# Second attention of a five-stage network: operations of the prologue reordered and moved between engines, reciprocals formed on ScalarE, the first sequence's tensors stored in six transfers

## The chip, the core and the metric

The kernel runs on one core of a Trainium2 chip. Its engines work side by side, each through its own list of instructions, and wait for each other by semaphores: TensorE (PE; its weight loads are PEld), VectorE (DVE), ScalarE (ACT), GpSimd (POOL) and SyncE (SP), which here only issues DMAs. TensorE's clock is granted at 1.2 or 2.4 GHz, in the profile 0.5 or 1. The metric is the device time of one execution, in microseconds.

## The reference, cut to what matters

The network computes, on x of shape (4, 1024, 128), attention a, a feed-forward block, attention b, a second feed-forward block with the same weights, each on a layer norm of x and added to x. The change is in attention b (16 heads of 8 channels, 4 sequences of 1024 tokens):

```python
Q, K, V = (split_heads(jnp.einsum('bsd,od->bso', x, W)) for W in (Wq, Wk, Wv))
Q, K = _apply_rope(Q, cos, sin), _apply_rope(K, cos, sin)
logits = jnp.einsum('bhnd,bhmd->bhnm', Q, K) * scale
probs = jax.nn.softmax(jnp.where(causal, logits, -jnp.inf), axis=-1)
attn = jnp.einsum('bhnm,bhmd->bhnd', probs, V).swapaxes(-3, -2).reshape(*x.shape[:-1], D)
return jnp.einsum('bsd,od->bso', attn, Wo)
```

## The kernel before

`network` runs five stages one after the other; `attn_b_stage` is the third. X lies in SBUF with the 128 channels on the partitions and 4 x 1024 tokens along them.

**Norm.** X is normed in eight chunks c of 512 tokens, two to a sequence b: TensorE centres (`centre`, L1527), ScalarE squares (L1727), TensorE averages (`mean`, L1536), ScalarE forms the reciprocal root by a logarithm and an exponential (`rstd`, L1733, L1735), VectorE multiplies (`normed`, L1845). Two banks alternate.

**Q and K.** For each sequence b and w (0 is Q, 1 is K) four products (`product`, L1549) give the projection and that of the swapped channels, i = 0 and 1, into two banks of 1024 columns. The rope is two multiplications by tables and an addition. For b = 0 VectorE does them from PSUM (L1853, L1856); for b = 1, 2, 3 ScalarE first copies the banks to SBUF (`hold`, L1753; into TA and TB, for b = 2 into XN and XE) and GpSimd multiplies and adds (`turn_and_add`, L1966, L1969). The sum is cut into three bf16 parts: first part a copy by ScalarE (L1740), remainder (L1861 or L1975), second part by ScalarE (L1744), third part (L1866 or L1980). `store_parts` (L1461) writes all three to DRAM by one DMA per tensor, and `load(m)` (L1471, L1476) brings group m of four heads back, three DMAs for each of QS and KS, into a ring of three. `value_product` (L1557) gives V, copied by ScalarE (L1758).

**Scores twice.** There are 16 groups m, four to a sequence. First each query's maximum is found: max units on TensorE (L1606 mask, L1609 scores) into two banks, reduced by VectorE (L1884). When the maximum of a group is known (L1894), GpSimd splits it (`offsets`, L2002 to L2008), TensorE turns it (L1618), VectorE casts it (L1901), SyncE writes it into QS as three further rows (`rows`, L1496). Then exp units compute the transposed scores with that offset (L1635, L1640), ScalarE takes the exponential (L1816), and the value products (L1655) sum outputs and denominators. Step n, 0 to 15, has eight slots j: exponentials of group n, tiles j, with maxima of group n + 1 (slots 0 to 3) and n + 2 (slots 4 to 7) between. The cast of group n + 1 is in slot 5 of step n; the casts mark the steps below. During steps -2 and -1, where there are only maxima, the 18 projection pieces of sequences 2 and 3 lie between them.

**Output.** ScalarE copies each half output to OS (`copy_out`, L1805), and `store_out` moves numerators (L1489, into OA) and denominators (L1491, into DA) by 8 small DMAs into the place of the rope tables; for the first two sequences it waits until all rope work is done (L1485). Step 4b + 5 closes sequence b: four reciprocals of 256 columns (`denominators`, L1907), two scalings (`scale`, L1912), two output products (L1664), added to X (L1919). Sequence 3 is closed behind the last step.

The order within each engine is written by hand: the calls at the end of each engine's block.

## Time and profile before

| | us |
|---|---|
| median of 3 runs | 2334.87 (2330.69 to 2345.4) |
| the profiled execution | 2331.8 |
| its span, first to last instruction | 2330.0 |
| TensorE busy (matmuls) | 2106.8 |
| VectorE busy | 1815.8 |
| ScalarE busy | 1386.5 |
| GpSimd busy | 1175.6 |

The second attention lies at about 915 to 1587 us of the span. In the rows further down a time in brackets is how long the engine stood idle before the row, and the arrow names what ended that; "x8" is the number of instructions that a row gathers; SPq is SyncE's issue of DMAs.

### The profile page before, as it was taken

The page shows a single profiled execution, that of the slowest core. Times are in us where ns is not written, and L with a number is a line of the kernel's source. Part 1 is how long each engine was busy: PE and PEld are TensorE (multiplying, and loading weights), DVE is VectorE, ACT ScalarE, POOL GpSimd, SP SyncE. Part 2 cuts the span into 40 slices and gives each one's busy share as a digit, 9 for nine tenths or more (in the row PEclk, how much of TensorE's full clock was granted, in tenths as well). Part 3 has the DMA queues.
Part 4 walks back from the last instruction along what each step waited for, and adds up shares of the span by engine and source line. Part 5 has one row for each costly group of instructions (what it writes and reads, how often), then busy time and mean ns, then how long its engine had stood idle before and what let it go on. Part 6 is the DMA issues. An engine that isn't in the chain of part 4 may idle for free. (4 is left out here: it accounts for less than half of the span.)

```text
span 2330.0 us, 45158 instructions
## 1 busy us (share of the span) xinstructions
PE 2106.8 (90%) x16918; PEld 1085.9 (47%) x16918; DVE 1815.8 (78%) x2394; ACT 1386.5 (60%) x3463; POOL 1175.6 (50%) x533
## 2 busy tenths in 40 slices
PE   5687899999999998787999989996899999999997
PEld 2233555555555553332333333333455555555553
...
GB/s 60 0 1 82 69 33 42 42 33 46 33 42 42 33 33 51 89 54 31 74 51 33 47 49 44 35 12 78 71 37 37 43 36 44 37 35 45 34 36 42
DMA packets 85564, 101.16 MB, mean 43 GB/s; under 512 B 13305, under 2 KB 59329, under 8 KB 83045
## 3 DMA queue, kind: packets, MB, share of 16 engines
q1 hardware_dynamic: 82981, 96.64, 15.6%
q8 instruction: 137, 2.24, 0.4%
...
## 5 line engine op out<-in xcount | busy, mean ns | idle before, releaser
L831 POOL TENSOR_TENSOR ffn_RN<-ffn_SS,ffn_mhalf 128x16 f32<-128x16 f32 x128 | 372.5, 2910 | 282.3 <-DVE ffn_SS L777 281.8
L1884 DVE TENSOR_REDUCE attn_b_NX<-attn_b_s 128x1 f32<-128x512 f32 (+3 forms) x608 | 384.4, 659 | 152.9 <-PE attn_b_s L1609 148.5
L1816 ACT ACTIVATE attn_b_PT<-attn_b_s 128x1024 f32<-128x1024 f32 (+3 forms) x352 | 298.3, 870 | 237.3 <-PE attn_b_s L1640 232.7
L825 POOL TENSOR_TENSOR ffn_QK<-ffn_T 128x1024 f32<-128x1024 f32 x128 | 421.4, 3292 | 19.9 <-DVE ffn_T L725 19.6
L576 ACT ACTIVATE ffn_PB<-ffn_s,ffn_NM 128x128 f32<-128x128 f32 x1024 | 359.9, 385 | 102.2 <-DVE ffn_NM L747 102.2
L612 ACT ACTIVATE ffn_SQ<-ffn_w 128x1024 f32<-128x1024 f32 x128 | 131.0, 1024 | 311.8 <-DVE ffn_T L725 311.5
L819 POOL TENSOR_TENSOR ffn_PB<-ffn_PB,ffn_RDEN 128x1024 f32<-128x1024 f32 x128 | 243.7, 1904 | 23.7 <-DVE ffn_RDEN L710 23.7
L367 PE MATMUL ffn_w<-ffn_Wqkv,ffn_H 128*128 128x512 f32 x512 | 245.4, 602 | 9.1 <-ACT ffn_SQ L612 5.6
L1609 PE MATMUL attn_b_s<-attn_b_KS,attn_b_QS 72*128 72x512 bf16 (+3 forms) x768 | 223.8, 339 | 12.8 <-DVE attn_b_NX L1884 9.7
L576 ACT ACTIVATION_READ_ACCUMULATOR ffn_PB<-ffn_s,ffn_NM 128x1 f32 x1024 | 230.9, 225 | 0.0
L741 DVE TENSOR_TENSOR ffn_QK<-ffn_QK,ffn_RN 128x1024 f32<-128x1024 f32 x128 | 221.4, 1730 | 0.4 <-POOL ffn_RN L831 0.3
L764 DVE COPY ffn_PT<-ffn_w 128x1024 f32<-128x1024 f32 x128 | 156.2, 1220 | 75.1 <-PE ffn_w L421 71.7
L442 PE MATMUL ffn_m<-ffn_HN,ffn_W 128*114 128x512 f32 x360 | 185.9, 613 | 6.6 <-ACT ffn_G L596 4.1
L1640 PE MATMUL attn_b_s<-attn_b_QS,attn_b_KS 75*128 75x512 bf16 (+3 forms) x768 | 190.3, 337 | 0.0
L722 DVE TENSOR_TENSOR ffn_T<-ffn_w,ffn_rope 128x1024 f32<-128x1024 f32 x128 | 154.8, 1210 | 36.3 <-PE ffn_w L367 36.1
L1655 PE MATMUL attn_b_o<-attn_b_PT,attn_b_VQ 128*32 128x512 f32 (+3 forms) x1536 | 170.7, 517 | 0.1
L747 DVE TENSOR_REDUCE ffn_NM<-ffn_s 128x8 f32<-128x1024 f32 x128 | 155.5, 1215 | 11.5 <-PE ffn_s L409 11.5
L725 DVE TENSOR_TENSOR ffn_T<-ffn_w,ffn_rope 128x512 f32<-128x512 f32 x256 | 163.6, 681 | 0.0
L774 DVE TENSOR_REDUCE ffn_SS<-ffn_SQ 128x16 f32<-128x1024 f32 x128 | 154.6, 1208 | 2.2 <-ACT ffn_SQ L612 2.2
L437 PEld LDWEIGHTS ffn_w<-ffn_PT,ffn_Voff 128*64 128x64 f32 x2048 | 107.3, 137 | 101.1 <-issue 94.6
L421 PEld LDWEIGHTS ffn_w<-ident,ffn_PB 128*128 128x128 f32 x1024 | 116.5, 142 | 74.8 <-issue 60.2
L367 PEld LDWEIGHTS ffn_w<-ffn_Wqkv,ffn_H 128*128 128x128 f32 x512 | 95.0, 193 | 117.3 <-issue 82.4
(242 smaller groups left out, 3801.0 us busy)
## 6 DMA issues: line engine op xcount, KB each, us to landing
...
attn_b_rope<-attn_b_OS SPq DMA_DIRECT2D x256, 16.0 KB
```

The source lines that it names most:

```text
L367: last = pe.matmul(w0_ps[:, c, :], H1[:, g % 2, b, :], Wqkv[:, l, c, :], start=True, stop=True)
L442: pe.matmul(mlp_bank(g, half, j), W1[:, g // NT, half, j, :], HN[:, :], start=True, stop=True)\
L576: last = act.activation(PB[:, x % 2, e, p, :], s_ps[:, e, p * P:(p + 1) * P], ACT.Exp, bias=NM[:, x % 2, e, p:p + 1], accum_out=DEN[:, x % ...
L741: dve.tensor_tensor(qk, qk, RN[:, x % 2, :].unsqueeze(2).broadcast_to([P, 2 * NH, DH]), ALU.mult)\
L819: pool.tensor_tensor(probs_x, probs_x, by, ALU.mult).then_inc(normed, 1)
L825: pool.tensor_tensor(QK[:, x % 2, :, :, :].rearrange("p c q k -> p (c q k)"), T1[:, :, :, :].rearrange("p c h k -> p (c h k)"), T2[:, :, : ...
L831: pool.tensor_tensor(RN[:, x % 2, :], SS[:, x % 2, :], mhalf[:, :], ALU.pow).then_inc(rnorm, 1)
L1609: last = pe.matmul(bank[:, q * width:(q + 1) * width], QS[0:KS9, m % RING, g + q, i * P:(i + 1) * P], KS[0:KS9, m % RING, g + q, lo:hi], s ...
L1640: last = pe.matmul(bank[:, q * pitch + lo:q * pitch + hi], KS[:, n % RING, g + q, j * P:(j + 1) * P], QS[:, n % RING, g + q, j * P + lo:j ...
L1655: last = pe.matmul(o_ps[half][VCOLS * g:VCOLS * (g + 1), lo - half * 512:512], VQ[:, n % 2, g, j, :], PT[:, j % 2, g, lo - j * P:hi - j * ...
L1816: act.activation(PT[:, j % 2, g:g + pack, 0:width], s2_ps[k % 2][:, 0:pack * pitch].rearrange("p (q w) -> p q w", q=pack)[:, :, 0:width], ...
L1884: dve.tensor_reduce(NX[:, m % 2, c, g:g + pack, i], s1_ps[k % 2][:, 0:pack * (hi - lo)].rearrange("p (q w) -> p q w", q=pack), AX_X, ALU.m ...
```

## The change

The diff, cut to its core (adapted thresholds of waits are left out, except in `store_out`):

```diff
+    def store_part(b, w, a):
+        sp.wait_ge((p1, p2, p3)[a], 2 * b + w + 1)
+        sp.dma_start(qk_dram[w][a, b * P:(b + 1) * P, :], RP[:, w, a, :]).then_inc(s_parts_out[w], 16)
...
         else:
-            sp.wait_ge(turned, 8)
-            sp.wait_ge(rotated, 4 * (NB - 1))
+            sp.wait_ge(turned, 16)
+            sp.wait_ge(rotated, 4 * (NB - 2))
         cols = slice(half * 512, (half + 1) * 512)
         for g in range(BG):
-            to = slice(n % 4 * 32 + g * BD, n % 4 * 32 + (g + 1) * BD)
-            sp.dma_start(OA[to, b % 2, cols], OS[32 * g:32 * g + BD, n % 2, cols])\
+            sp.dma_start(DA[rows_of(n, g), b % 2, cols], OS[32 * g + BD:32 * g + 2 * BD, n % 2, cols])\
               .then_inc(s_back[half][n % 2], 16)
-            sp.dma_start(DA[to, b % 2, cols], OS[32 * g + BD:32 * g + 2 * BD, n % 2, cols])\
-              .then_inc(s_back[half][n % 2], 16)
+        if (n, half) != (NG - 1, 1):
+            for g in range(BG):
+                sp.dma_start(OA[rows_of(n, g), b % 2, cols], OS[32 * g:32 * g + BD, n % 2, cols])\
+                  .then_inc(s_back[half][n % 2], 16)
...
-    for w in range(2):
-        store_parts(0, w)
+    for a in range(PARTS):
+        for w in range(2):
+            store_part(0, w, a)
     for m in range(RING):
...
     rows(0)
-    for w in range(2):
-        store_parts(2, w)
     for n in range(NG):
...
             store_out(n - 1, 1)
-        if n + 1 < NG:
-            rows(n + 1)
-        store_out(n, 0)
         if n == 2:
...
                 store_parts(3, w)
+        if n + 1 < NG:
+            rows(n + 1)
+        if n >= 1:
+            store_out(n, 0)
         if n + RING < NG:
...
             load(n + RING)
+        if n == 0:
+            for w in range(2):
+                store_parts(2, w)
+            store_out(0, 0)
     store_out(NG - 1, 1)
...
         pe.wait_ge(s_w, 16 * WLOADS)
-        pe.wait_ge(n_ln, min(2 * b + 4, NCH))
+        pe.wait_ge(n_ln, NCH if b else 4)
         wait(pe, v_copied, 2 * b)
...
         mean(c)
-    projections(0, 0)
+    projections(0)
     for c in range(2, 4):
         centre(c)
-    projections(0, 1)
+    projections(1)
     for c in range(2, 4):
...
     value_product(0)
-    for c in range(4, 6):
+    for c in range(4, 8):
+        w, h = divmod(c - 4, 2)
         centre(c)
-    projections(1, 0)
-    for c in range(4, 6):
+        for i in range(2):
+            product(1, w, i, h)
         mean(c)
-    projections(1, 1)
-    for c in range(6, 8):
-        centre(c)
     value_product(1)
-    for c in range(6, 8):
-        mean(c)
     pe.wait_ge(n_out, NCH)
...
         square(c)
-    for c in range(2, 4):
-        rstd(c)
+    rstd(2)
     first_part(0, 1)
...
         second_part(0, w)
+    rstd(3)
     copy_values(0)
-    for c in range(4, 6):
+    for c in range(4, 8):
         square(c)
-    for c in range(4, 6):
         rstd(c)
-    hold(1, 0)
-    hold(1, 1)
-    for c in range(6, 8):
-        square(c)
+    first_part(1, 0)
     copy_values(1)
-    for c in range(6, 8):
-        rstd(c)
+    first_part(1, 1)
     hold(2, 0)
     for w in range(2):
-        first_part(1, w)
+        second_part(1, w)
+    hold(2, 1)
     copy_values(2)
-    hold(2, 1)
-    for w in range(2):
-        second_part(1, w)
     for w in range(2):
...
     copy_values(3)
-    for w in range(2):
-        first_part(2, w)
     act.wait_ge(n_out, NCH)
...
+    def inverse(b, half):
+        cols = slice(half * 512, (half + 1) * 512)
+        for i in range(2):
+            act.wait_ge(s_back[half][i], 32 * BG * (2 * b + 2))
+        act.activation(DA[:, b % 2, cols], DA[:, b % 2, cols], ACT.Ln).then_inc(s_lden, 1)
+        act.wait_ge(s_lden, 2 * b + half + 1)
+        act.activation(DA[:, b % 2, cols], DA[:, b % 2, cols], ACT.Exp, scale=-1.0).then_inc(s_rden, 1)
...
                     for w in range(2):
+                        first_part(2, w)
+                if (n, j, g) == (0, 6, 0):
+                    for w in range(2):
                         second_part(2, w)
-                if (n, j, g) == (1, 1, 1):
+                if (n, j, g) == (1, 5, 0):
                     for w in range(2):
                         first_part(3, w)
-                if (n, j, g) == (2, 1, 1):
+                if (n, j, g) == (1, 7, 0):
                     for w in range(2):
                         second_part(3, w)
+                if n % 4 == 1 and n > 1 and j in (2, 3) and g == 0:
+                    inverse(n // 4 - 1, j - 2)
                 if (j, g) == (5, 0):
...
     copy_out(NG - 1, 1)
+    act.wait_ge(o_read[1], NG)
+    act.wait_ge(s1_mm, s1_at["out", NB - 3, 1] + 1)
+    for g in range(BG):
+        act.dma_start(OA[rows_of(NG - 1, g), (NB - 1) % 2, 512:], OS[32 * g:32 * g + BD, (NG - 1) % 2, 512:])\
+           .then_inc(s_back[1][(NG - 1) % 2], 16)
+    for half in range(2):
+        inverse(NB - 1, half)
...
+    def turn(b, w, i, h):
+        half = slice(h * 512, (h + 1) * 512)
+        dve.wait_ge(ab_mm, 8 * b + 4 * w + (2 * h + i if b else 2 * i + h) + 1)
+        wait(dve, p3, (w + 1) * b)
+        dve.tensor_tensor((TA, TB)[i][:, w, half], s2_ps[i][:, half], rope[:, 2 * w + i, half], ALU.mult)\
+           .then_inc(turned, 1)
...
         dve.wait_ge((s_wq, s_wk)[w], 16 * 4)
-        for i, dst in enumerate((TA, TB)):
+        for i in range(2):
             for h in range(2):
-                half = slice(h * 512, (h + 1) * 512)
-                dve.wait_ge(ab_mm, 4 * w + 2 * i + h + 1)
-                dve.tensor_tensor(dst[:, w, half], s2_ps[i][:, half], rope[:, 2 * w + i, half], ALU.mult)\
-                   .then_inc(turned, 1)
+                turn(0, w, i, h)
         dve.wait_ge(turned, 4 * w + 4)
...
         remainder(w)
+    normed(2)
     for w in range(2):
         third_part(w)
-    for c in range(2, NCH):
+    normed(3)
+    for c in range(4, NCH):
+        w, h = divmod(c - 4, 2)
+        for i in range(2):
+            turn(1, w, i, h)
         normed(c)
...
-    def denominators(b, lo, hi):
-        half = lo // 512
-        for i in range(2):
-            dve.wait_ge(s_back[half][i], 32 * BG * (2 * b + 2))
-        dve.reciprocal(DA[:, b % 2, lo:hi], DA[:, b % 2, lo:hi]).then_inc(s_rden, 1)
...
             for b in closing:
-                if 1 <= slot <= 4:
-                    denominators(b, 256 * (slot - 1), 256 * slot)
                 if slot in (5, 6):
                     scale(b, slot - 5)
-            if n == NG - 1 and slot == 6:
-                denominators(NB - 1, 0, 256)
-                denominators(NB - 1, 256, 512)
-                scale(NB - 1, 0)
         if n == NG:
-            denominators(NB - 1, 512, 768)
-            denominators(NB - 1, 768, 1024)
-            scale(NB - 1, 1)
+            for half in range(2):
+                scale(NB - 1, half)
         for b in range(NB):
...
+    def add(b, w, a, c):
+        pool.tensor_tensor(a, a, c, ALU.add).then_inc(rsum, 1)
...
     def turn_and_add(b, w):
-        pool.wait_ge((s_wq, s_wk)[w], 16 * 4)
-        k = 4 * (b - 1) + 2 * w
-        for i, at in enumerate(work_buffers(b, w)):
+        k = 4 * (b - 2) + 2 * w
+        a, c = work_buffers(b, w)
+        for i, at in enumerate((a, c)):
             pool.wait_ge(held, k + i + 1)
             pool.tensor_tensor(at, at, rope[:, 2 * w + i, :], ALU.mult).then_inc(rotated, 1)
-        a, c = work_buffers(b, w)
         pool.wait_ge(rotated, k + 2)
-        pool.tensor_tensor(a, a, c, ALU.add).then_inc(rsum, 1)
+        add(b, w, a, c)
...
     for w in range(2):
-        turn_and_add(1, w)
+        pool.wait_ge(turned, 8 + 4 * w + 4)
+        add(1, w, *work_buffers(1, w))
     parts_of(1)
-    for w in range(2):
-        turn_and_add(2, w)
+    turn_and_add(2, 0)
     for m in range(NG):
         offsets(m)
-        if m + 1 < NG:
-            values(m + 1)
         if m == 0:
+            values(1)
+            turn_and_add(2, 1)
+        elif m == 1:
             parts_of(2)
-        if m == 1:
             for w in range(2):
                 turn_and_add(3, w)
-        if m == 2:
-            parts_of(3)
+            values(2)
+        else:
+            if m == 2:
+                parts_of(3)
+            if m + 1 < NG:
+                values(m + 1)
```

TensorE takes chunks 4 to 7 one at a time, with two products of sequence 1 behind each centring, and the values of sequence 1 after the last mean. VectorE does the rope multiplications of sequence 1 itself; GpSimd only adds. In ScalarE's prologue the copies change places, and the copies of parts of sequences 2 and 3 now stand among the exponentials of steps 0 and 1.

On ScalarE, the order behind the chunks 2 and 3 of the norm (RP is the buffer of the parts, VB of the values). Before:

```order
L1733 ACTIVATE attn_b_PT<-attn_b_o,eps 128x512
L1735 ACTIVATE attn_b_PT<-attn_b_PT 128x512
L1733 ACTIVATE attn_b_PT<-attn_b_o,eps 128x512
L1735 ACTIVATE attn_b_PT<-attn_b_PT 128x512
L1740 ACTIVATE attn_b_RP<-attn_b_TA 128x1024
L1744 ACTIVATE attn_b_RP<-attn_b_TA 128x1024 x2
L1758 ACTIVATE attn_b_VB<-attn_b_o 128x4x4x32 x2
```

Now:

```order
L1743 ACTIVATE attn_b_PT<-attn_b_o,eps 128x512
L1745 ACTIVATE attn_b_PT<-attn_b_PT 128x512
L1750 ACTIVATE attn_b_RP<-attn_b_TA 128x1024
L1754 ACTIVATE attn_b_RP<-attn_b_TA 128x1024 x2
L1743 ACTIVATE attn_b_PT<-attn_b_o,eps 128x512
L1745 ACTIVATE attn_b_PT<-attn_b_PT 128x512
L1768 ACTIVATE attn_b_VB<-attn_b_o 128x4x4x32 x2
```

The root of chunk 3 has moved behind the three copies of parts.

On GpSimd, the work of sequence 2 (in XN and XE) around the offsets of group 0 (NP, NR). Before:

```order
L1966 TENSOR_TENSOR attn_b_XN<-attn_b_XN,attn_b_rope 128x1024 x2
L1969 TENSOR_TENSOR attn_b_XN<-attn_b_XN 128x1024
L1966 TENSOR_TENSOR attn_b_XE<-attn_b_XE,attn_b_rope 128x1024
L1966 TENSOR_TENSOR attn_b_XN<-attn_b_XN,attn_b_rope 128x1024
L1969 TENSOR_TENSOR attn_b_XE<-attn_b_XE,attn_b_XN 128x1024
L2002 TENSOR_TENSOR attn_b_NP<-attn_b_NM,attn_b_zeros 128x32
```

Now:

```order
L1986 TENSOR_TENSOR attn_b_XN<-attn_b_XN,attn_b_rope 128x1024 x2
L1979 TENSOR_TENSOR attn_b_XN<-attn_b_XN 128x1024
L2021 TENSOR_TENSOR attn_b_NP<-attn_b_NM,attn_b_zeros 128x32
L2023 TENSOR_TENSOR attn_b_NR<-attn_b_NM,attn_b_NP 128x32
L2025 TENSOR_TENSOR attn_b_NP<-attn_b_NR,attn_b_zeros 128x32
L2027 TENSOR_TENSOR attn_b_NP<-attn_b_NR,attn_b_NP 128x32
L2011 COPY attn_b_VQ<-attn_b_VB 128x8x4x8
L1986 TENSOR_TENSOR attn_b_XE<-attn_b_XE,attn_b_rope 128x1024
```

K's three operations have moved behind the offsets.

On SyncE, steps 0 and 1, now (before, the eight stores of group 0's first half output stood ahead of the loads, and sequence 2's parts ahead of both):

```order
L1504 DMA attn_b_QS<-attn_b_MT 3x32x128 x2
L1478 DMA attn_b_QS<-attn_b_qk_parts 24x1x4096 x3
L1483 DMA attn_b_KS<-attn_b_qk_parts 24x1x4096 x3
L1464 DMA attn_b_qk_parts<-attn_b_RP 128x3x1024 x2
L1495 DMA attn_b_rope<-attn_b_OS 8x512 x4
L1499 DMA attn_b_rope<-attn_b_OS 8x512 x4
...
L1504 DMA attn_b_QS<-attn_b_MT 3x32x128
```

The load of group 3 stands ahead of the stores into the rope tables; two half outputs are stored before the offsets of group 2.

## Rows read from the trace of the kernel before

**Rows 1.** The page's first line.

```profile
span 2330.0 us, 45158 instructions
```

**Rows 2.** Timeline 910 to 1012 us: start, duration, engine, line, operation, [idle before <-releaser].

```profile
933.84 0.67 ACT L1733 ACTIVATE attn_b_PT<-attn_b_o,eps 128x512 f32<-128x512 f32 x1
934.54 0.63 ACT L1735 ACTIVATE attn_b_PT<-attn_b_PT 128x512 f32<-128x512 f32 x1
...
934.65 2.02 PE L1557 MATMUL attn_b_o<-attn_b_Wv,attn_b_XN 128*128 128x128 f32 x16 [1.25 <-ACT attn_b_PT L1733]
935.08 1.04 ACT L1740 ACTIVATE attn_b_RP<-attn_b_TA 128x1024 bf16<-128x1024 f32 x1
...
940.38 3.54 PE L1527 MATMUL attn_b_s<-X,centre 128*128 128x512 f32 x4 [3.70 <-DVE attn_b_XN L1845]
...
943.75 3.60 PE L1549 MATMUL attn_b_s<-attn_b_XN,attn_b_W 128*128 128x512 f32 x8
...
947.18 1.88 PE L1536 MATMUL attn_b_o<-attn_b_PT,mean 128*128 128x512 f32 x4
...
964.82 0.23 PE L1606 MATMUL attn_b_s<-attn_b_causal,identb 128*128 128x128 bf16 x1 [2.55 <-DVE attn_b_XN L1845]
```

**Rows 3.** Timeline 969 to 1012 us, to the first exponential's mask matmul (last row).

```profile
985.23 1.10 PE L1549 MATMUL attn_b_s<-attn_b_XN,attn_b_W 128*128 128x512 f32 x2 [1.63 <-ACT attn_b_XE L1753]
...
998.28 2.35 DVE L1894 TENSOR_TENSOR attn_b_NM<-attn_b_NX 128x32 f32<-128x32 f32 x1
...
1002.96 2.34 POOL L1969 TENSOR_TENSOR attn_b_XE<-attn_b_XE,attn_b_XN 128x1024 f32<-128x1024 f32 x1
...
1006.62 0.31 PE L1618 MATMUL attn_b_s<-identb,attn_b_NP 128*96 128x128 bf16 x1 [3.71 <-POOL attn_b_NP L2008]
...
1011.02 0.31 PE L1635 MATMUL attn_b_s<-attn_b_causal,identb 128*128 128x128 bf16 x1
```

**Rows 4.** Stretches: length, busy us of PE, PEld, DVE, ACT, POOL; clock, DMA share, GB/s.

```profile
955.00:960.00 5.00, 4.06 (x22) 2.67 (x20) 0.00 (x0) 3.02 (x5) 4.92 (x3) 1.00 0.19 79
...
985.00:990.00 5.00, 4.20 (x15) 1.87 (x16) 2.60 (x5) 3.71 (x5) 2.98 (x2) 1.00 0.15 64
...
1010.00:1020.00 10.00, 9.90 (x35) 4.33 (x34) 5.67 (x9) 5.21 (x6) 0.97 (x1) 0.50 0.01 2
```

**Rows 5.** Timeline of steps 1 and 2, 1054 to 1125 us.

```profile
1066.10 1.06 ACT L1740 ACTIVATE attn_b_RP<-attn_b_TA 128x1024 bf16<-128x1024 f32 x1 [5.95 <-POOL attn_b_TA L1969]
...
1068.02 0.29 PE L1635 MATMUL attn_b_s<-attn_b_causal,identb 128*128 128x128 bf16 x1 [9.80 <-ACT attn_b_PT L1816]
...
1069.27 2.24 SPq L1471 DMA_DIRECT2D attn_b_QS<-attn_b_qk_parts  x3
...
1087.35 0.39 PE L1635 MATMUL attn_b_s<-attn_b_causal,identb 128*128 128x128 bf16 x2 [4.84 <-DMA attn_b_KS<-attn_b_qk_parts]
...
1100.15 0.60 ACT L1816 ACTIVATE attn_b_PT<-attn_b_s 128x512 f32<-128x512 f32 x1 [0.97 <-PE attn_b_s L1640]
...
1101.07 0.22 PE L1635 MATMUL attn_b_s<-attn_b_causal,identb 128*128 128x128 bf16 x1
```

**Rows 6.** Stretches from cast to cast of the offsets (L1901), columns as in rows 4.

```profile
1095.40:1127.60 32.20, 31.41 (x243) 12.51 (x242) 24.38 (x41) 21.01 (x27) 9.76 (x9) 1.00 0.15 47
1193.50:1233.40 39.90, 35.11 (x245) 13.38 (x242) 30.55 (x45) 20.77 (x27) 1.39 (x5) 0.91 0.12 38
1333.60:1371.00 37.40, 32.00 (x244) 12.39 (x242) 30.31 (x45) 20.64 (x27) 1.38 (x5) 1.00 0.13 40
1469.70:1511.20 41.50, 37.85 (x244) 14.44 (x242) 30.43 (x45) 20.51 (x27) 1.39 (x5) 0.84 0.11 36
1041.80:1095.40 53.60, 38.39 (x245) 14.12 (x242) 24.85 (x42) 21.38 (x28) 15.29 (x11) 0.81 0.09 28
```

**Rows 7.** Timeline of the tail, 1565 to 1600 us.

```profile
1577.47 0.62 SPq L1491 DMA_DIRECT2D attn_b_rope<-attn_b_OS  x1
...
1579.53 3.36 DVE L1907 RECIPROCAL attn_b_rope<-attn_b_rope 128x256 f32<-128x256 f32 x2 [1.30 <-DMA attn_b_rope<-attn_b_OS]
```

30 lines of the change are left out of this document (17 added, 13 removed).

## The prediction

> **What bounds the kernel now.** I read the page's head first (a span of 2330.0 us; the run took 2331.8, so 1.8 us lie around it) [rows 1]. Only one of five stages is touched, the second attention, about 915 to 1587 us. There I read the timeline stretch by stretch, each time for the wait that ends last. It falls into four pieces. (a) A prologue: the norm's chunks travel ScalarE to VectorE to TensorE and back, and TensorE waits 3.70 us for the third chunk and 2.55 us for the last one; it begins the first scores at 964.8 us [rows 2]. (b) From there to the first exponential at 1011.0 us: the maximum of group 0 is started at 998.28, but GpSimd is in the middle of six multiplications and additions of sequence 2 and is free only at 1005.3 us, so TensorE waits 3.71 us for the offsets [rows 3]. (c) Sixteen steps. An ordinary one takes 32.2 us with TensorE busy for 31.41 of them [rows 6]: TensorE bounds it, and whatever makes it wait is lost. Step 0 to 1 takes 53.6 us instead [rows 5]: TensorE stands 9.80 us because ScalarE waits for GpSimd's sum of sequence 3, and 4.84 us for the load of group 3. Those are one chain: SyncE may store group 0's output over the rope tables only when GpSimd has finished with them, and the load (issued at 1069.27) is queued behind those stores [rows 5]. (d) Three closing steps with four reciprocals of 1.7 us on VectorE each, and a tail behind the last stores [rows 6, 7].
>
> **The change part by part.** Times below are times of the old trace, moved.
>
> Prologue. ScalarE: the second half of the reciprocal roots of chunk 3 (a logarithm and an exponential, 0.67 + 0.63 us) no longer stands before the first part of K, which started at 935.08 [rows 2]; it starts when the roots of chunk 2 end, 933.9. The chain of first part, VectorE's remainder, second part and third part then ends near 938.1 (Q) and 939.3 (K) instead of 938.5 and 939.7. Chunk 2 is normed between, at 936.9. The price is that the values of sequence 0 now wait for chunk 3's logarithm: TensorE's idle time is 4.65 us (933.4 to 938.05), then 2.0 us of values, and the fifth chunk's centring starts at 940.1, where it started at 940.38 [rows 2]. From there the two schedules differ. Per chunk TensorE now has one centring, two products and one mean, four pieces like the four products that now start at 943.75 and are followed 3.43 us later (947.18) by the means [rows 2]: 3.43 us. ScalarE has three operations and VectorE three per chunk, of 0.6 to 0.7 us each (2.1 at most), so TensorE bounds it: 4 x 3.43 = 13.7 us. The clock is granted at half speed after the idle time of 3.70 us now (two centrings took 3.54 us at 940.38, two means 1.88 at full speed [rows 2]), and I keep that loss of 1.7 us. Last mean at 940.1 + 13.7 + 1.7 = 955.5; the values of sequence 1 wait 0.75 us for the last logarithm and take 2.0: first scores at 958.3. Now 964.8: a gain of **6.5 us**. VectorE's eight rope multiplications replace four evacuations of 1.0 us on ScalarE and four multiplications of 2.35 us on GpSimd.
>
> Cover that can be gone: the scores need the load of group 0. Loads move at 79 GB/s, 0.19 of the DMA capacity, until 985 to 990 us, when the rate falls [rows 4]; they are issued from 942.1, so three take 47 us, one 15.6, and group 0 is there at 957.7, if they land in order; at the latest at 964.5, since nothing waited for it. The six small stores should let it start 1.3 us earlier (last part on its way at 939.3, a third of the bytes). Needed at 958.3: 1.9 us to spare, or 4.9 us short at the far bound (964.5 - 1.3 - 958.3). I take nothing, since the nearest reading is the measured rate.
>
> To the first exponential. The evacuation of sequence 2's K now stands before the copy of its values (1.1 us), and TensorE's 1.63 us wait for it [rows 3] shrinks by that. GpSimd now has only three operations of sequence 2 between the parts of sequence 1 (done near 973) and the offsets: it is idle when the maximum is ready. So the maximum starts at 998.3 - 6.5 - 1.1 = 990.7, and need not take 2.35 us for its 32 elements, an operation that now overlaps GpSimd's; five reductions of some 0.65 us later, at 993.8, TensorE turns the offsets, and it reaches the first exponential 4.4 us after that, as now (1006.62 to 1011.02): 998.2 [rows 3]. Gain so far **12.8 us**.
>
> Step 0 ran at half clock for most of its first 12 us (0.50 from 1010 to 1020 [rows 4]). From the first exponential to the next cast it took 30.8 us (1011.0 to 1041.8); at full clock the same stretch takes 26.5 (from 1101.07 [rows 5] to the cast at 1127.6 that ends the first window of rows 6). Gain **4.3**, together 17.1.
>
> Step 1. GpSimd after the change: sequence 2's third parts end 9.2 us after cast 1 (that cast now at 1024.7), six operations of 2.35 us end at 1048; ScalarE needs the sum at 1057, 9 us later: no wait. SyncE issues the load of group 3 at 1031, ahead of the stores: landed by about 1050 (18 us from issue to the end of the wait now, 1069.3 to 1087.35 [rows 5]), needed at 1053. So 53.6 becomes 32.2: gain **21.4**. The stores of two half outputs (16 issues of 0.62 [rows 7] and a little between them, 10.7 us from 1045.5) end at 1056.2, and the offsets' row of group 2 is queued behind them and wanted at 1057.
>
> What is moved onto ScalarE costs something. Two copies (2.1 us) beside the exponentials were free in step 2: they stand in the window of 32.2 us whose ScalarE time is 21.01 [rows 6]. But now pairs stand at the end of steps 0 and 1, where the idle time before an exponential is 0.97 us [rows 5]: 2.1 - 0.97 = 1.1, of which step 0 loses perhaps half, and in step 1 a second pair delays the head pair of tile 5 too. I take 0.5 + 1.7 = **2.2 us lost** (bounds 0 and 4.4).
>
> Closing steps. They take 39.9, 37.4 and 41.5 us [rows 6]; against 32.2 the three lose 22.1 us. Reciprocals alone are 4 x 1.7 = 6.8 each; the rest is half clock in two of them (0.91, 0.84 [rows 6]). Now ScalarE does two logarithms and two exponentials, 2 x (0.67 + 0.63) = 2.6 us [rows 2], the size of the pair that was free. Bounds: nothing, and 2.6 each; I take 0.8 each, so the gain is 22.1 - 2.4 = **19.7** (14.3 to 22.1). The closing's other half (scalings, output product) stays.
>
> A rule against this change: the Trainium skill (DMA: Bandwidth & Descriptors, section Bandwidth) advises transfers of at least 1 MiB and measures 138 GB/s at 64 KB; at that rate a 256 KB part takes 1.9 us. By it the sum changes by at most the 1.3 us of earlier start, which lies in the cover; no row of the kernel before shows a transfer of that size.
>
> Tail. Two reciprocals (3.36 us) follow the last of eight store issues (1577.47; they begin 2.06 us later, when it has landed) [rows 7], and a scaling of 0.7 ends at 1583.6. Four of the issues go to ScalarE's queue, so SyncE's last comes 4 x 0.65 = 2.6 us earlier; logarithm and exponential (1.3) replace 3.36. Gain 2.6 + 2.0 = **4.6**.
>
> Sum: 17.1 + 21.4 - 2.2 + 19.7 + 4.6 = 60.6, and 2331.8 - 60.6 = 2271.2. The run of the profile lies 3.1 us under the median shown (2334.87), which one long run raises; I forecast 2272.
>
> **The rivals.** (1) ScalarE's insertions cost what they last: 4.4 and 2.6 x 3 instead of 2.2 and 2.4, so 7.6 us less gain: about 2280. For it: an exponential that comes late delays the value product behind it. Against: the window of 32.2 with 21.01 us of ScalarE [rows 6]. (2) The clock: TensorE's idle time ahead of the values grows to 4.65 us, and half speed stays or returns where I have it full, in the chunks (1.7 us more), in step 0 (4.3) and in one closing (4.1, the third over the second, 41.5 - 37.4): about 2282. (3) The load of group 0 is the bound: up to 4.9 us: 2277. (4) The queue behind the moved stores: if GpSimd runs 3.9 us later than I have it, the offsets' row of group 2 is late, and each further us is lost; ten later would be 6: 2278. (5) The change doesn't remove the reciprocals' cost, since TensorE waits for its score banks anyway: then 19.7 falls away, 2292. Against it: ordinary steps take 32.2 and the middle closing, at full clock, 5.2 more. (6) Slower: the new mix keeps TensorE at 1.2 GHz through the steps. In step 0, 12 us at half clock cost 4.3, so they did 7.7 us of work, and a whole step of 32.2 would take 50; it decides from three and a half steps on (60.6 / 18), and with five the kernel is 1% slower, 2361. Rows 6 show a whole step at 1.00, which is against it.
>
> **How the numbers follow.** As forecast 0.63; (1) 0.13, (2) 0.10, (3) 0.05, (4) 0.03, (5) 0.04, (6) 0.02. The range goes from 2260 (no insertion costs anything, 4.6 off; the half clock of the chunks gone too, 1.7; the closings that follow a half-clocked one also freed of it, some 4) to 2289, which leaves out (5), (6) and a sum of (1) with (2). A change of 1%, 23 us, is about what a measurement of this kernel can tell from none. Faster by over 1% (under 2311.5): 0.95; within 1%: 0.03; slower: 0.02.
>
> **What the profile after would show.** First scores at 958, first exponential at 998, cast 1 at 1025, cast 2 at 1057.5; maximum 0 of 0.19 us; no wait of TensorE over 2 us in step 1; closing windows of 32 to 35 us at clock 1.00; the tail's last scaling 4.6 us earlier relative to the last exponential. I am wrong if the first scores wait for a DMA, if step 1 is still above 36 us, or if the closings keep more than 4 us each.

## The result, and the profile after

Over four executions the changed kernel has a median of 2275.18 us (2273.19 to 2283.85); the kernel before, timed beside it, 2339.16 (2330.69 to 2345.4). The ratio is 0.9736, 95% interval 0.9692 to 0.9779: 2.2 to 3.1% faster. Forecast were 2272 us and a range of 2260 to 2289.

The first profile of the changed kernel happened to be its longest execution (2283.85), so I took a second one (`r1_again`, 2275.14; six executions, median 2275.32). Their heads:

```profile
span 2282.1 us, 45155 instructions
PE 2099.0 (92%) x16918; PEld 1085.6 (48%) x16918; DVE 1792.8 (79%) x2386; ACT 1391.9 (61%) x3475; POOL 1166.3 (51%) x529
```

```profile
span 2273.3 us, 45155 instructions
PE 2091.5 (92%) x16918; PEld 1084.1 (48%) x16918; DVE 1792.4 (79%) x2386; ACT 1391.8 (61%) x3475; POOL 1166.1 (51%) x529
```

Same instructions, and TensorE busy 7.5 us longer in the first: that is clock, not work. The stage also begins at a slightly different time in each execution, because the stages ahead of it vary. So every mark below is counted from the stage's own first centring (915.78 us before, 918.62 and 917.14 in the two profiles after), and the stage ends where GpSimd clears its first tile of the next one (1587.75, 1538.31, 1529.15).

| from the stage's start, us | before | after, 1st | after, 2nd | gain, 2nd | forecast |
|---|---|---|---|---|---|
| first scores | 49.0 | 44.1 | 43.9 | 5.1 | 6.5 |
| scores for the first exponential | 95.2 | 84.9 | 84.7 | 10.5 | 12.8 |
| cast 1 | 126.1 | 115.7 | 115.5 | 10.5 | 17.1 |
| cast 2 | 179.6 | 147.9 | 147.8 | 31.8 | 38.5 |
| cast 3 | 211.8 | 187.2 | 181.0 | 30.8 | |
| cast 15 | 627.9 | 578.7 | 572.5 | 55.4 | |
| end of the stage | 672.0 | 619.7 | 612.0 | 60.0 | 60.6 |

The sum came out in the second profile, its terms didn't all: several missed by 1 to 4 us, in both directions. Over the first profile the stage gained 52.3 us. The other stages took 1658.0 us of the span before and 1661.3 in the second profile, with not one instruction changed there; over all 14 profiles of this study they take 1655.9 to 1662.4. That is 3.3 of the 3.9 us by which the second profile's execution lies above 2271.2; the other 0.6 are the stage's.

The windows of the first profile after, by cast as in [rows 6] (columns: start:end, length, busy time of PE, PEld, DVE, ACT and POOL, TensorE's granted clock, DMA share, GB/s). They are step 0, step 1, step 2, and the three steps in which the first closings fall:

```profile
999.40:1034.30 34.90, 33.46 (x199) 13.07 (x199) 24.43 (x41) 18.33 (x21) 8.19 (x8) 0.80 0.01 2
1034.30:1066.60 32.30, 31.42 (x244) 12.55 (x242) 24.48 (x42) 21.28 (x28) 21.03 (x14) 1.00 0.27 95
1066.60:1105.90 39.30, 37.61 (x244) 14.09 (x242) 24.55 (x42) 23.09 (x30) 9.81 (x9) 0.83 0.23 79
1170.30:1202.80 32.50, 31.53 (x245) 12.55 (x242) 24.50 (x42) 21.58 (x30) 1.38 (x5) 1.00 0.14 46
1301.40:1333.80 32.40, 31.43 (x243) 12.56 (x242) 24.39 (x41) 21.48 (x29) 1.39 (x5) 1.00 0.15 47
1432.50:1464.90 32.40, 31.43 (x244) 12.56 (x242) 24.40 (x42) 21.48 (x30) 1.38 (x5) 1.00 0.14 46
```

Read the clock (third from the right) first. Step 1 (53.60 before, now 32.30) and the closings (39.90, 37.40, 41.50, now 32.4 to 32.5) are at 1.00, with TensorE busy for all but 0.9 to 1.0 us: they are ordinary steps now. Step 0 is at 0.80 and as long as before (34.9). Step 2 is at 0.83 here and takes 39.30; in the second profile the same instructions take 33.30 at clock 1.00:

```profile
1064.90:1098.20 33.30, 31.48 (x244) 12.55 (x242) 24.46 (x42) 23.03 (x30) 9.77 (x9) 1.00 0.27 94
```

### The profile page after: what moved, and what is told of

It is laid out like the page before. It is cut to its first block and busy times, and to the rows that moved or that the text cites. A ratio compares the mean times of both kernels' runs of the same rounds, so it can differ in the third digit from the quotient of the medians.

```text
span 2282.1 us, 45155 instructions
## 1 busy us (share of the span) xinstructions
PE 2099.0 (92%) x16918; PEld 1085.6 (48%) x16918; DVE 1792.8 (79%) x2386; ACT 1391.9 (61%) x3475; POOL 1166.3 (51%) x529
## 5 line engine op out<-in xcount | busy, mean ns | idle before, releaser
L1619 PE MATMUL attn_b_s<-attn_b_KS,attn_b_QS 72*128 72x512 bf16 (+3 forms) x768 | 219.1, 334 | 5.8 <-DVE attn_b_NX L1914 2.5
L367 PEld LDWEIGHTS ffn_w<-ffn_Wqkv,ffn_H 128*128 128x128 f32 x512 | 95.2, 193 | 120.0 <-issue 82.6
```

The source lines that it names most:

```text
L367: last = pe.matmul(w0_ps[:, c, :], H1[:, g % 2, b, :], Wqkv[:, l, c, :], start=True, stop=True)
L1619: last = pe.matmul(bank[:, q * width:(q + 1) * width], QS[0:KS9, m % RING, g + q, i * P:(i + 1) * P], KS[0:KS9, m % RING, g + q, lo:hi], s ...
```

## The experiments

Each is one edit of the changed kernel unless said otherwise. They ran in three groups on the same chip, each beside the kernel before: the first four below (kernel before 2329.34 us); the reciprocals, the two transfers, the stores ahead of the load and the two fillings together (2330.88); the filling in the kernel before, the later GpSimd, the third filling and the load in pieces (2328.88). Where a time is compared with the changed kernel's, that is its median of 2275.32 from the first group.

### The same kernel once more

> The changed kernel as it is, a second profile of it. The first one lay 8.7 us over its own median (2283.85 against 2275.18) and shows TensorE at half clock in two stretches of the steps, 1001.6 to 1015.2 us (step 0) and 1076.7 to 1090.3 us (end of step 2's first tiles; cast 2 to cast 3 took 39.30 us where an ordinary step takes 32.24). Theory A: the half clock belongs to what the engines do there, so both stretches come back at the same places (within 1 us of the casts beside them), and the windows cast 0 to 1 and cast 2 to 3 are again 34.9 and 39.3 us. Theory B: the two stretches are chance; then a profile near 2275 us lacks one of them, and its window is 32.2 to 32.5 us. Median 2275 us in either.

Median 2275.32, ratio 0.9763 (0.9736 to 0.979). Half clock of step 0: there again (14 us, from 1.4 us behind cast 0); half clock of step 2: absent. So both theories hold, one for each place. With the runs below, step 0 took 34.8 to 35.7 us in all nine profiles whose TensorE has nothing added ahead of it (the kernel before among them), while step 2, in seven with the pair of copies in tile 7 of step 1, took 33.25 three times, 36.19, 36.20, 36.32, and 39.30. (The eighth with that pair is the run with GpSimd later, whose step 2 holds a further wait.)

### Second parts of sequence 3 later

```diff
-                        if (n, j, g) == (1, 7, 0):
+                        if (n, j, g) == (2, 1, 1):
                             for w in range(2):
                                 second_part(3, w)
```

> Only ScalarE's second parts of sequence 3 move, from tile 7 of step 1 to tile 1 of step 2, where the kernel before had them (the pair lasts 1.99 us; behind it TensorE waited 0.96 us at 1075.01 and went to half clock 1.7 us later, for 13.6 us). Theory A (ScalarE's pair behind the last tile is what makes TensorE stand, and the standing brings the half clock): cast 2 to cast 3 falls from 39.3 to 32.3 us and the kernel to 2268. Theory B (the pair costs what it lasts, the half clock comes from something else): the window loses 1 to 2 us at most, the half clock stays near 1077, the kernel 2274. Theory C (the pair in tile 1 meets the load and stores there): the window stays or grows.

Median 2271.4, 3.9 us under the changed kernel; the intervals of the two ratios overlap (0.9718 to 0.9776 here), so the windows must tell it. What the pair does in tile 7 shows in the second profile of the changed kernel (ScalarE, then TensorE; start, duration, and in brackets the idle time and what ended it):

```profile
1070.42 1.99 ACT L1754 ACTIVATE attn_b_RP<-attn_b_TA 128x1024 bf16<-128x1024 f32 x2
...
1073.38 0.23 PE L1645 MATMUL attn_b_s<-attn_b_causal,identb 128*128 128x128 bf16 x1 [0.95 <-ACT attn_b_PT L1825]
```

The pair stands in front of the next step's exponentials and TensorE stands 0.95 us. Moved by two tiles it has slack: step 2 takes 32.5 us, at full clock, in this and in the three other profiles with the pair there.

```profile
1063.80:1096.30 32.50, 31.45 (x244) 12.55 (x242) 24.43 (x42) 22.88 (x30) 9.76 (x9) 1.00 0.28 96
```

Theory A, with a correction: the pair costs 0.8 us each time, and in four of seven profiles a stretch of half clock follows, 2.9 to 6.1 us more. Against the second profile, which lacks that stretch, the move gains only the 0.8 us of theory B.

### Two more such pairs, and a third at the end

```diff
+                        if (n, j, g) in ((6, 7, 0), (10, 7, 0), (14, 7, 0)):
+                            for w in range(2):
+                                act.wait_ge(s_parts_out[w], 16 * (3 + PARTS))
+                                act.activation(RP[:, w, 1, :], TA[:, w, :], ACT.Copy)
```

> The changed kernel with work added: in steps 6, 10 and 14 ScalarE does, behind the exponential of tile 7, two more copies of 128x1024 into a buffer that nothing uses any more (the same 1.99 us at the same place as the second parts of sequence 3 in step 1). Theory A (such a pair there stops TensorE about 1 us and brings the half clock): the windows of casts 7 to 8, 11 to 12 and 15 on, 32.24 us each now, grow by 7 us each where the next step is whole, in all 14 to 21 us: about 2290. Theory B (a pair costs its wait only, the half clock has another cause): 0 to 1 us each, about 2277.

Median 2282.7, 7.4 us over the changed kernel: neither theory's number. The windows behind the first two of the added pairs:

```profile
1226.20:1262.10 35.90, 34.38 (x244) 13.44 (x242) 24.53 (x42) 21.08 (x28) 1.39 (x5) 0.90 0.13 42
1360.90:1393.90 33.00, 31.35 (x244) 12.55 (x242) 24.41 (x41) 21.20 (x27) 1.39 (x5) 1.00 0.14 46
```

One with a stretch of half clock (3.7 us over the ordinary 32.24), one without (0.8 us); the stretch from cast 15 to the stage's end is 3.7 longer than in the second profile, but some half clock comes there without a pair too (1.5 us in the first profile of the changed kernel). The same edit at the same place: a short stand of TensorE sometimes brings the half clock and sometimes not. No run here shows what decides it.

### Work for TensorE ahead of step 0

```diff
                             max_unit(m, *unit)
+                            if n == -1 and m == 1:
+                                pe.wait_ge(held, 4 * (NB - 2))
+                                for _ in range(2):
+                                    pe.matmul(s2_ps[0][:, 0:512], QS[0:KS9, 0, 0, 0:P], KS[0:KS9, 0, 0, 0:512],
+                                              start=True, stop=True, skip_group_check=True)
```

> The changed kernel with work added: behind each of the eleven score units of group 1 ahead of step 0, TensorE does two more products of 512 columns (0.22 us each at full clock) into a bank that the first exponential's scores overwrite. Nothing reads them. Between 995 and 1003 us TensorE was busy 3.7 to 4.4 of each 5 us, and its clock fell to half at 1001.6. Theory A (low work of TensorE ahead of step 0 brings its half clock): the half clock of step 0 goes, cast 0 to cast 1 falls from 34.9 to 31 or 32 us, less up to 2 us that the added products delay the score units; 2272 to 2275. Theory B (the half clock is set by something else, such as a fixed time behind the last one): cast 0 to cast 1 stays at 34.9 or grows by up to 3 us; 2275 to 2280.

(The added lines stand here in place of a helper.) Median 2268.86, 6.5 us under the changed kernel. First the 9 us of the second profile that end where its step 0 fell to half clock (999.2 us), and 9 us from some 30 us earlier; then the 9 us of this run that correspond to the first, and its step 0:

```profile
990.20:999.20 9.00, 7.31 (x44) 3.95 (x43) 6.93 (x14) 2.11 (x3) 5.15 (x7) 1.00 0.08 32
958.00:967.00 9.00, 6.80 (x38) 4.09 (x39) 4.89 (x8) 4.86 (x7) 6.16 (x3) 1.00 0.19 79
```

```profile
987.00:996.00 9.00, 8.53 (x55) 5.07 (x54) 6.71 (x14) 2.11 (x3) 5.80 (x7) 1.00 0.05 19
994.10:1024.20 30.10, 29.02 (x207) 11.74 (x207) 24.26 (x42) 17.71 (x22) 8.06 (x8) 1.00 0.01 2
```

TensorE busy for 8.53 instead of 7.31 of the 9 us, the other engines about as they were, and step 0 takes 30.1 us instead of 34.9. Theory A: filling the gaps takes the half clock away. That little busy time alone brings it is not shown, and the second line speaks against it: around 958 us TensorE was busy for 6.80 of 9 us, and its clock stayed full until 999.2. The score units were not delayed (cast 0 came 80.2 us from the stage's start, 80.6 without). The step in which I had expected 4.3 us from the clock held 4.8, and the change had not touched what brings them.

### The same in the kernel before

```diff
+                            if n == -1 and m == 1:
+                                filler(2)
...
                         if slot == TURN_SLOT and n == -1:
+                            filler(14)
                             turn_unit(0)
```

`filler(k)` is the same product k times.

> The kernel before with the same filling of TensorE ahead of step 0: two added products behind each of the eleven score units of group 1 and 14 ahead of the turning of group 0's offsets, where it stood 3.71 us. Theory A (step 0's half clock belongs to TensorE's idle time ahead of it, in both kernels, and the change neither made nor removed it): cast 0 to cast 1 falls from 34.87 to 30 or 31 us and the kernel gains 4 to 5 us. Theory B (in the kernel before something else lowers the clock in step 0): the window stays at 34.9 and nothing is gained.

```profile
1001.40 3.18 PE L1670 MATMUL attn_b_s<-attn_b_KS,attn_b_QS 72*128 72x512 bf16 x14
1005.09 0.23 PE L1618 MATMUL attn_b_s<-identb,attn_b_NP 128*96 128x128 bf16 x1 [0.51 <-POOL attn_b_NP L2017]
```

```profile
1005.40:1035.20 29.80, 28.86 (x206) 11.59 (x204) 24.17 (x41) 17.72 (x22) 9.26 (x8) 1.00 0.15 55
1035.20:1089.50 54.30, 39.84 (x244) 14.86 (x242) 24.77 (x41) 21.30 (x28) 15.29 (x11) 0.75 0.09 28
```

Step 0 falls from 34.87 to 29.8 us, as theory A has it: in this kernel too the half clock goes when the time ahead is filled. This run fills the gaps and the wait of 3.71 us together, so it doesn't say which of them brings the half clock in the kernel before. And the kernel gains only 1.1 us between the medians (ratio 0.9981, 0.9962 to 1.0), not the 4 to 5 of theory A, and not told from nothing. The profile shows where the 5 us go: the window of step 1 is 0.8 us longer than before, the first two closings 2.3 and 2.4, the step behind the second closing 1.6, while the third closing (3.0) and the step behind the first (1.6) are shorter; the half clock behind the waits falls differently.

### Reciprocals back on VectorE

```diff
-                        if n % 4 == 1 and n > 1 and j in (2, 3) and g == 0:
-                            inverse(n // 4 - 1, j - 2)
...
+                        if 1 <= slot <= 4:
+                            denominators(b, 256 * (slot - 1), 256 * slot)
...
```

The four reciprocals behind the last step are put back likewise.

> The changed kernel with VectorE's reciprocals back: four of 128x256 in each closing step and four at the end instead of ScalarE's logarithms and exponentials; everything else as changed. Theory A (my sum: the reciprocals cost 19.7 us in the closings beyond what ScalarE's way costs; by the windows of both profiles it would be 23.2: 39.88, 37.42 and 41.55 against 32.43 each): the windows of casts 5 to 6, 9 to 10 and 13 to 14 are 37 to 42 us again, with half clock near one or two of them, the tail 2 to 3 us longer, the kernel 2294 to 2300. Theory B (TensorE waited for its banks anyway, the reciprocals cost little): windows within 1 us of 32.4, kernel 2278.

Median 2300.61, ratio 0.9864 (0.9839 to 0.9889): the stage takes 635.8 us, 23.8 more than in the second profile. The three closing windows:

```profile
1162.70:1201.70 39.00, 33.56 (x244) 12.87 (x242) 30.40 (x46) 20.71 (x27) 1.39 (x5) 0.96 0.12 39
1300.30:1340.20 39.90, 35.11 (x244) 13.35 (x242) 30.55 (x46) 20.77 (x27) 1.40 (x5) 0.91 0.11 38
1440.40:1477.80 37.40, 31.98 (x244) 12.38 (x242) 30.32 (x45) 20.63 (x27) 1.40 (x5) 1.00 0.12 40
```

VectorE is busy 6 us longer than in the same windows after (30.4 against 24.4 to 24.5) and does four instructions more, reciprocals of 1.74 us each; at full clock that costs 5.0 us a step, and 6.6 and 7.4 where the half clock follows. Together with 1.6 in the step behind the second closing that is 20.6, and 3.2 in the tail. Theory A; its 2294 to 2300 us for the kernel was missed by 0.6.

### Two transfers for the first sequence

```diff
-            for a in range(PARTS):
-                for w in range(2):
-                    store_part(0, w, a)
+            for w in range(2):
+                store_parts(0, w)
```

> The changed kernel with the first sequence's parts stored in two transfers of 768 KB in all three parts again, each behind its third part, instead of six of one part. Theory A (my prediction: the load of group 0 starts 1.3 us later and has about 2 us of cover): the first scores start 0 to 1 us later, the kernel is within 1 us of 2275. Theory B (the first scores wait for the load; in the first profile of the changed kernel they did so for 0.68 us): they start 1.3 us or more later, up to 4 if the large transfers land later, and the kernel is 2276 to 2279.

Median 2276.48 (2275.31 to 2281.9), ratio 0.9766 (0.9744 to 0.9789): not to be told from the changed kernel by time. The profile tells it. First scores and load of group 0 in the changed kernel (first profile), then here:

```profile
944.85 2.32 SPq L1478 DMA_DIRECT2D attn_b_QS<-attn_b_qk_parts  x3
962.70 0.22 PE L1616 MATMUL attn_b_s<-attn_b_causal,identb 128*128 128x128 bf16 x1 [0.68 <-DMA attn_b_KS<-attn_b_qk_parts]
```

```profile
942.36 2.32 SPq L1474 DMA_DIRECT2D attn_b_QS<-attn_b_qk_parts  x3
960.50 0.22 PE L1611 MATMUL attn_b_s<-attn_b_causal,identb 128*128 128x128 bf16 x1 [2.51 <-DMA attn_b_KS<-attn_b_qk_parts]
```

With this stage's start at 914.58 the load is issued 27.8 us from it, against 26.2 in the first profile of the changed kernel and 24.2 in most others (see below), and TensorE waits 2.51 instead of 0.68 us. Theory B: in this one profile the first scores come 45.9 us from the start, against 43.1 to 44.1 with six transfers, so these are worth 1.8 to 2.8 us there. This profile also has a further stretch of half clock behind that wait (its cast 0 comes 4.7 us later), which its median does not show. That the third parts' stores land later in some executions is taken up in the part on the prediction.

### Stores ahead of the load

```diff
                 if n + 1 < NG:
                     rows(n + 1)
-                if n >= 1:
-                    store_out(n, 0)
+                store_out(n, 0)
```

> The changed kernel with one place of the store queue as before: group 0's first half output is stored ahead of the load of group 3, not behind it; GpSimd's order stays the new one. The stores over the rope tables may start when GpSimd's last multiplication of sequence 3 ends, about 21 us after cast 1, so the load is issued 26 us after cast 1 and landed 18 us later, where TensorE wants it about 20 us after cast 1. Theory A (order of the queue is needed beside GpSimd's earlier finish): one wait of TensorE for the load of 20 to 25 us, cast 1 to cast 2 of 52 to 60 us instead of 32.2, kernel 2295 to 2303. Theory B (GpSimd's late sum alone made step 1 long): 32 to 36 us, kernel within 4 us of 2275.

Median 2292.67, ratio 0.9834 (0.981 to 0.9858). SyncE, TensorE and the window:

```profile
1057.57 2.24 SPq L1478 DMA_DIRECT2D attn_b_QS<-attn_b_qk_parts  x3
...
1075.78 0.39 PE L1643 MATMUL attn_b_s<-attn_b_causal,identb 128*128 128x128 bf16 x2 [17.27 <-DMA attn_b_KS<-attn_b_qk_parts]
...
1031.20:1084.60 53.40, 35.35 (x244) 13.56 (x242) 24.54 (x41) 21.33 (x28) 21.05 (x14) 0.81 0.17 58
```

The one line of the queue brings back the whole of step 1: 53.4 us against 53.60 before [rows 6], with one wait of 17.27 us for the load where there were 9.80 for GpSimd's sum and 4.84 for the load [rows 5]. GpSimd was done in time here and that alone gained nothing in this step. Theory A, at the low end of its numbers (a wait of 17.27 us for 20 to 25, a kernel of 2292.67 for 2295 to 2303). The reverse, the new queue with GpSimd's old order, was not run.

### GpSimd later in step 1

```diff
                     parts_of(2)
+                    for k in range(4):
+                        pool.tensor_tensor(XN[:, 1, :], XN[:, 1, :], XN[:, 0, :], ALU.add).then_inc(s_extra, 1)
+                        pool.wait_ge(s_extra, k + 1)
                     for w in range(2):
                         turn_and_add(3, w)
```

> The changed kernel with work added: four more additions of 128x1024 on GpSimd (2.35 us each, 9.4 in all) ahead of its rope work of sequence 3 in step 1. My prediction gave GpSimd 3.9 us of cover there, since the offsets' row of group 2 is queued behind the stores that wait for GpSimd; the second profile of the changed kernel shows that row issued at 1065.22, right behind the cast at 1064.91 and the store before it. Theory A (that queue is the limit, with next to no cover left): the first scores of step 2 wait for the row, 8 to 10 us lost, 2283 to 2288 us, with half clock behind the wait. Theory B (the cover is as large as predicted): 5 to 6 us lost, 2281. Theory C (no one waits): 2275.

Median 2281.52, 6.2 over the changed kernel. Ahead of step 2 and in it:

```profile
1063.33 0.23 PE L1629 MATMUL attn_b_s<-identb,attn_b_NP 128*96 128x128 bf16 x1 [2.85 <-POOL attn_b_NP L2028]
...
1070.22 0.77 SPq L1505 DMA_DIRECT2D attn_b_QS<-attn_b_MT  x1
...
1073.22 0.22 PE L1646 MATMUL attn_b_s<-attn_b_causal,identb 128*128 128x128 bf16 x1 [2.07 <-DMA attn_b_QS<-attn_b_MT]
...
1063.60:1103.90 40.30, 37.52 (x246) 14.47 (x243) 24.48 (x40) 20.92 (x25) 9.34 (x9) 0.83 0.25 81
```

TensorE stands twice: 2.85 us for GpSimd's offsets, which I had not thought of, and 2.07 us for the offsets' row, which is issued behind the stores as forecast. The four additions took 9.7 us and bring 4.9 us of waits, so some 4.7 us were cover. The median is theory B's; but the windows of steps 1 and 2 (34.84 and 40.32 us) are together 9.7 longer than in the second profile, which is theory A's size, and 3.6 longer than in the first. The run doesn't decide between A and B; theory C is out. The rest of step 2's length is half clock.

### Both fillings and the later pair together

The added products ahead of step 0, the later pair, and while TensorE stands for the logarithm of chunk 3:

```diff
+                if b == 0:
+                    pe.wait_ge(turned, 8)
+                    for _ in range(18):
+                        pe.matmul(s2_ps[0][:, 0:512].rearrange("p (q w) -> p q w", q=4), keep["identb"][:, :],
+                                  causal[:, 0:1, :].broadcast_to([P, 4, P]), start=True, stop=True)
+                    pe.wait_ge(n_ln, 4)
```

(The number stands in place of its name; the wait for the norm that stood ahead now applies to the later sequences only.)

> What the first four runs point to, put together: second parts of sequence 3 in tile 1 of step 2 (its window 32.49 instead of 33.25), the added products behind group 1's score units (step 0: 30.09 instead of 34.89 us), and 18 more added products of 512 columns while TensorE stands 4.5 us for the logarithm of chunk 3, ahead of the values of sequence 0, into a bank that nothing holds then. Theory A (work keeps the clock, here too): the values take 2.0 instead of 3.75 us, the chunks behind them 3.43 us each from the first on, the first scores start 1.5 to 3.4 us earlier against the stage's start unless they then wait for the load of group 0; kernel 2262 to 2266. Theory B (at this place the half clock comes anyway, or the load of group 0 holds the scores): first scores where they were, kernel 2267 to 2268.

Median 2263.35 (2261.23 to 2264.9), ratio 0.9706 (0.9685 to 0.9727): 12 us under the changed kernel's 2275.32, measured in another group. The values of sequence 0 after the change, here, and this kernel's first scores:

```profile
940.79 3.75 PE L1571 MATMUL attn_b_o<-attn_b_Wv,attn_b_XN 128*128 128x128 f32 x16 [4.54 <-ACT attn_b_PT L1743]
```

```profile
936.07 2.05 PE L1579 MATMUL attn_b_o<-attn_b_Wv,attn_b_XN 128*128 128x128 f32 x16 [0.57 <-ACT attn_b_PT L1760]
...
955.81 0.22 PE L1624 MATMUL attn_b_s<-attn_b_causal,identb 128*128 128x128 bf16 x1 [1.11 <-DMA attn_b_KS<-attn_b_qk_parts]
```

Theory A, to the point where the load takes over: the values run at full clock (2.05 us instead of 3.75), the first scores come 41.8 us from the stage's start instead of 43.9, and now wait 1.11 us for the load.

### A third filling, and the load of group 0 in pieces

Both stand on the kernel with both fillings. The first adds, in `output_unit`,

```diff
+                if (b, half) == (NB - 1, 0):
+                    for _ in range(26):
+                        pe.matmul(s2_ps[0][:, 0:512], QS[0:KS9, 0, 0, 0:P], KS[0:KS9, 0, 0, 0:512], start=True,
+                                  stop=True, skip_group_check=True)
```

and the second besides, on SyncE (`load_q` is one load of QS, which waits for its own part alone)

```diff
             for a in range(PARTS):
                 for w in range(2):
                     store_part(0, w, a)
-            for m in range(RING):
+                if a == 1:
+                    load_q(0, 0)
+            for a in range(1, PARTS):
+                load_q(0, a)
+            load_k(0)
+            for m in range(1, RING):
                 load(m)
```

> The kernel with both fillings (2263.35 us) with a third: while TensorE stands 6.62 us ahead of the last output products, it does 26 more products of 512 columns into a bank that nothing reads any more. There the output products ran at half clock (3.94 us for two of 512 columns), and the norm's first centring of the next stage too (3.75 us). Theory A (work keeps the clock): the output products take 2.0 us, of which 1 us lies on the path, the first centring 2.0 instead of 3.75; kernel 2 to 3 us faster, 2260.5 to 2261.5. Theory B (the wait of 2 us between the stages is enough to bring half clock): only the 1 us of the output product, 2262.5.

> As the run before it, and the three loads of group 0's Q are issued one by one, each behind the store of its own part (the first ahead of the stores of the third parts), where all six loads stood behind all six stores. In the kernel with both fillings the first scores waited 1.11 us for the load. Theory A (the loads share a bandwidth of 79 GB/s, so what starts earlier lands earlier): the wait goes, 1.1 us gained. Theory B (a load ahead of the third parts' stores delays these, or K's three loads set the end): the wait stays within 0.5 us or grows.

Medians 2267.1 and 2266.91, ratios 0.9719 (0.969 to 0.9747) and 0.9717 (0.9691 to 0.9743): neither can be told from 0.9706, and neither is shown to gain. The third filling does what it is for: each output product takes 1.10 us, where two took 3.94,

```profile
1516.54 1.10 PE L1686 MATMUL attn_b_s<-attn_b_rope,attn_b_Wo 128*128 128x512 f32 x2 [0.91 <-DVE attn_b_rope L1957]
```

and 0.9 us come back between the first scaling and the last addition to X (this row gathers the two matmuls of one output product). But the next stage's first centring took 3.75 us as before, behind 2 us of standing between the stages (theory B), and this profile had a stretch of half clock in the last exponentials that took 1.5 us. The load in pieces changed nothing: the first scores waited 1.08 us instead of 1.11. Its first load was issued 2.4 us sooner, but K's loads, which need all three parts of K, were issued 29.5 us from the stage's start instead of 26.5: theory B, whose price (the third parts' stores held up) and gain cancel here.

## Why the prediction was right, and where its steps were not

**First scores: 5.1 instead of 6.5 us.** The steady part was right: the means lie 3.43 us apart (947.85, 951.29, 954.72, 958.15 in the first profile). Two terms were off. I booked 1.7 us of half clock behind TensorE's wait for chunk 3; it was 2.6, for the values of sequence 0 took 3.75 us instead of 2.0 and the first centring behind them 1.9 instead of 1.0. That is half of what rival (2) had for the chunks. The other is the load of group 0. VectorE's third parts are done 23.2 us from the stage's start (23.9 in the kernel before). In the two profiles of the changed kernel and in the run with the reciprocals back, the load was still issued only at 26.1 to 26.4, as in the kernel before (26.3), and TensorE waited 0.6 to 0.7 us for it: rival (3), at a seventh of the 4.9 us that it could have been, and my first sign of being wrong. In the five other profiles with this prologue the load was issued at 24.2 and no one waited for it, as in the run with the later pair:

```profile
941.09 2.32 SPq L1478 DMA_DIRECT2D attn_b_QS<-attn_b_qk_parts  x3
...
960.06 0.22 PE L1616 MATMUL attn_b_s<-attn_b_causal,identb 128*128 128x128 bf16 x1
```

There the first scores came at 43.1 to 43.3 us, a gain of 5.7 to 5.9. The same program's store of Q's third part landed 1.7 us behind its issue in one case (near the 1.9 of my estimate) and 3.6 to 3.9 in the other; what decides it no run shows. Where TensorE waited for the load, it took 17.6 to 17.9 us from its issue, not the 15.6 that I worked out from 79 GB/s. So the cover was 1.4 us in five profiles (1.9 forecast) and gone in three. Two transfers instead of six cost 1.6 or 3.6 us at the load, by the case they are held against (1.3 forecast).

**To the first exponential: 5.4 more instead of 6.3.** The mechanism held: GpSimd waits for the maximum of group 0 instead of the other way round, and the maximum has no more than its own time,

```profile
995.16 0.19 DVE L1924 TENSOR_TENSOR attn_b_NM<-attn_b_NX 128x32 f32<-128x32 f32 x1
```

where it took 2.35 beside GpSimd [rows 3]. From its start to the turning of the offsets it took 3.9 us where I had 3.1. No run takes the new order of the prologue back, so the 10.5 us up to here are read from the traces and not tested one by one.

**Step 0: nothing instead of 4.3 us. This step failed.** I took the half clock of step 0 as belonging to the wait of 3.71 us for the offsets [rows 3], which the change removes, and so counted full clock. The wait went (0.20 us are left) and the half clock stayed: 34.9 us again. Ahead of it TensorE still waits at the score units for VectorE, 0.2 to 0.5 us at a time, and was busy for 7.31 of 9 us. Given work in these gaps it kept its clock in every one of the four profiles of the changed kernel so filled, and the step took 30.1 us. So the single long wait was not needed. Why TensorE kept full clock at 958 to 967 us, busy for 6.80 of 9, is open. The sentence of rival (2), "half speed stays or returns where I have it full", named this place; its share of the chances, 0.10, was too small for this part of it.

**Step 1: 21.3 against 21.4.** Right, and it needs the queue's order: with the stores ahead of the load all of it is lost again. No wait of TensorE over 2 us is left there. My cover for GpSimd (3.9 us until the row of group 2 is late) was about right (some 4.7), but GpSimd's own splitting of the offsets is late too when it is delayed by 9.7.

**ScalarE's insertions: 1.0 us, and in some executions 2.9 to 6.1 more, against 2.2.** The size without the clock lies within my bounds of 0 and 4.4. What I left out is that a stand of 0.95 us there can be followed by half clock: at this place rival (1) brings rival (2) with it.

**Closings: 21.6 us, and 1.6 in the step behind the first, against 19.7.** Logarithm and exponential cost ScalarE's slack only: 32.43 us against 32.24, so 0.2 each where I took 0.8. Rival (5), that nothing is won, is refuted by the run with the reciprocals back (20.6 us in the same windows).

**Tail: 4.56 against 4.6.** From the end of the last exponential to the end of the last scaling it was 13.4 us (1570.21 to 1583.6; the last exponential of the kernel before stands here, what follows it in [rows 7])

```profile
1569.61 0.60 ACT L1816 ACTIVATE attn_b_PT<-attn_b_s 128x512 f32<-128x512 f32 x1 [0.31 <-PE attn_b_s L1640]
```

and is 8.85 (1516.17 to 1525.02 in the second profile):

```profile
1515.57 0.60 ACT L1825 ACTIVATE attn_b_PT<-attn_b_s 128x512 f32<-128x512 f32 x1 [0.31 <-PE attn_b_s L1650]
...
1517.34 3.66 ACTq L1855 DMA_DIRECT2D attn_b_rope<-attn_b_OS  x4
1518.75 2.62 SPq L1495 DMA_DIRECT2D attn_b_rope<-attn_b_OS  x4
1521.10 0.63 ACT L1806 ACTIVATE attn_b_rope<-attn_b_rope 128x512 f32<-128x512 f32 x1 [3.79 <-issue]
...
1524.33 0.69 DVE L1936 TENSOR_TENSOR attn_b_rope<-attn_b_rope 128x512 f32<-128x512 f32 x1 [1.21 <-ACT attn_b_rope L1808]
```

The sum was right by luck, for its split was wrong: the run with the reciprocals back is 3.2 us longer there, so logarithm and exponential are worth 3.2 and not 2.0, and what is left for the divided stores is some 1.4 and not 2.6. The four issues take ScalarE 0.92 us each, SyncE 0.66, and the first logarithm stands behind them.

**A gain that I had not listed:** the step from cast 3 to cast 4 took 33.67 us before and takes 32.24: 1.4 us. Before, TensorE stood there for a load of K,

```profile
1156.19 0.28 PE L1635 MATMUL attn_b_s<-attn_b_causal,identb 128*128 128x128 bf16 x2 [1.26 <-DMA attn_b_KS<-attn_b_qk_parts]
```

and no such wait is left.

Summed over the second profile: 10.5 (first exponential) + 0 (step 0) + 21.3 - 1.0 + 1.4 + 21.6 + 1.6 + 4.6 = 60.0. So the agreement with 60.6 is in part luck: 4.3 us too much at step 0 and 2.3 before it were met by 1.9 and 1.6 at the closings, 1.4 at cast 4 and 1.2 at the insertions. And it is the second profile's: with the half clock of step 2 the first gained 52.3. What was right in mechanism and size are step 1 and the closings, 43 of the 60 us.
